# A decoder layer on one core: context column sums made during the K projections, a correction added by VectorE, and another order of issue in the last head pair

## The reference, cut to what matters

```python
x = x + attn(layernorm(x), Wq, bq, Wk, bk, Wv, bv, Wo, bo, gq, gk)   # x: 2 x 256 x 512, 32 heads of 128
# second part: both sides are quantised, then multiplied
q1 = fake_quant(layernorm(x), x1_scale, x1_zp)     # (clip(round(v/s + z), 0, 255) - z) * s
q2 = fake_quant(ctx_4096, x2_scale, x2_zp)         # ctx_4096: 2 x 512 x 512
x = x + matmul(q1, q2)
# third part: base product, router over 15, top 8, eight low-rank experts
x = x + ffn(layernorm(x), base_W, base_b, router_W, router_b, A, B, expert_map)
```

## Time and profile before

| | us |
|---|---|
| median of 3 runs | 529.79 (529.35 to 529.89) |
| the profiled execution | 529.43 |
| its span in the profile | 527.5 |
| PE busy in the span | 516.9 |
| last pair starts on PE | 474.2 |
| last projection of the last pair ends on PE | 493.85 |
| variance of tiles 2 and 3 ready on DVE | 495.70 |
| longest wait of PE behind 474 us | 0.78 |
| low_rank(0) starts on PE | 504.7 |
| last sum on DVE ends | 525.4 |

### The profile page before, as it was taken

One profiled execution on the slowest core, in us unless ns is written; L12 is line 12 of the kernel. 1 busy time (PEld: TensorE's weight loads), 2 busy tenths in 40 slices (PEclk: granted clock), 3 DMA queues, 4 the chain that ended last, 5 costly groups with the idle time before them and its releaser, 6 DMA issues.

```text
span 527.5 us, 9751 instructions
## 1 busy us (share of the span) xinstructions
PE 516.9 (98%) x3195; PEld 459.4 (87%) x3197; DVE 331.9 (63%) x701; ACT 355.4 (67%) x748; POOL 265.1 (50%) x223
## 2 busy tenths in 40 slices
PE   7999999999999999999999999999999999999897
PEld 6888888888888889999999999999999999997586
DVE  6354433276666777666766667666666667767875
ACT  4666666656666767777767777677777777776650
POOL 3344444464445545564656546465464655643350
PEclk9999999999999999999999999999999999999999
DMA  6444635333333121112221111211233312221002
GB/s 185 140 140 153 224 86 174 99 82 101 97 99 99 60 83 56 50 56 61 60 60 51 49 60 60 60 58 42 60 108 96 139 42 61 60 61 41 1 1 81
DMA packets 23496, 43.43 MB, mean 82 GB/s; under 512 B 3633, under 2 KB 3889, under 8 KB 23217
## 3 DMA queue, kind: packets, MB, share of 16 engines
q1 hardware_dynamic: 23472, 43.13, 27.1%
HBM read 41.03 MB, written 2.10 MB: 82 GB/s over the span
## 4 chain that ended last, share of the span: by engine, by line
PE 89%; DVE 5%; ACT 2%; DMA 2%; POOL 1%; issue 0%; SPq 0%; DVEq 0%; ACTq 0%
PE p_v L624 5%; PE p_o L551 5%; PE p_o L549 5%; PE p_o L550 5%; PE p_v L626 5%; PE p_v L625 5%; PE p_t L549 5%; PE p_t L551 5%; PE p_t L550 5%; PE acc L638 5%; PE acc L639 5%; PE acc L640 5%; PE p_t L610 5%; PE p_o L669 3%; PE p_o L671 3%; PE p_o L670 3%
## 5 line engine op out<-in xcount | busy, mean ns | idle before, releaser
L1205 DVE TENSOR_TENSOR w_lo<-raw,w_hi 128x512 fp32r<-128x512 f32 x64 | 44.2, 690 | 78.5 <-ACT w_hi L784 78.5
L1074 POOL TENSOR_TENSOR wo_lo<-raw,wo_hi 128x512 fp32r<-128x512 f32 x31 | 40.2, 1297 | 100.3 <-ACT wo_hi L939 97.1
L861 ACT ACTIVATE probs<-p_s,nbias,rq_t 128x256 f32<-128x256 f32 x128 | 71.2, 560 | 19.4 <-DVE nbias L1305 19.4
L784 ACT CAST w_hi<-raw 128x512 fp32r<-128x512 f32 x64 | 39.9, 624 | 61.0 <-PE p_o L551 29.8
L624 PE MATMUL p_v<-w_hi,xnt_hi 128*128 128x256 f32 x256 | 77.3, 302 | 0.0
L626 PE MATMUL p_v<-w_hi,xnt_lo 128*128 128x256 f32 x256 | 72.3, 282 | 0.0
L625 PE MATMUL p_v<-w_lo,xnt_hi 128*128 128x256 f32 x256 | 72.2, 282 | 0.0
L1056 POOL TENSOR_TENSOR acc_k<-acc_k,square 128x512 f32<-128x512 f32 x32 | 41.6, 1299 | 50.8 <-ACT square L799 50.8
L1056 POOL TENSOR_TENSOR acc_q<-acc_q,square 128x512 f32<-128x512 f32 x32 | 44.3, 1385 | 39.2 <-ACT square L799 38.9
L915 ACT CAST pt_hi<-p_t 128x512 fp32r<-128x512 f32 x64 | 37.4, 584 | 37.7 <-PE p_t L610 37.7
L1074 POOL TENSOR_TENSOR w_lo<-raw,w_hi 128x512 fp32r<-128x512 f32 x32 | 44.8, 1401 | 23.3 <-ACT w_hi L845 23.3
(11 more groups left out here) (286 smaller groups left out, 1473.6 us busy)
## 6 DMA issues: line engine op xcount, KB each, us to landing
raw<-in_wv SPq DMA_DIRECT2D x36, 256.0 KB, 2.6
raw<-in_wk SPq DMA_DIRECT2D x32, 256.0 KB, 2.6
raw<-in_wq SPq DMA_DIRECT2D x32, 256.0 KB, 2.6
raw<-in_wo SPq DMA_DIRECT2D x31, 256.0 KB, 2.6
ctx_f<-in_ctx SPq DMA_DIRECT2D x4, 512.0 KB, 3.7
xin<-in_x SPq DMA_DIRECT2D x4, 256.0 KB, 3.3
xb<-in_x SPq DMA_DIRECT2D x4, 256.0 KB, 5.5
ctx_kept<-ctx_k SPq DMA_DIRECT2D x1, 1024.0 KB, 4.7
```

What stands on the lines that cost most here:

```text
L861: act.activation(probs[:, n, a, :], p_s[:, a, :], ACT.Exp, bias=nbias[:, n, a:a + 1], scale=rq_t[:, 2 * b + a:2 * b + a + 1], accum_out=rs ...
L1074: pool.tensor_tensor(dst, raw[:, slot, :], hi, ALU.subtract).then_inc(w_lo_pool, 1)
L1205: dve.tensor_tensor(w_lo[:, n, 0:NC * DH], raw[:, r, :], w_hi[:, n, 0:NC * DH], ALU.subtract).then_inc(w_lo_dve, 1)
```

## The change

- During the K projections DVE adds the quantised context in pairs of row blocks (`sum_ctx`, 6 adds in all, in its left-over time), and the four `seed_acc` steps move behind them. After the last K unit PE makes the column sums with one matmul per batch (`ones_r` times `ctx_sum`), DVE scales them (`make_corr`) between its first two `weights_lo` of Q, and SP writes them to HBM (`corr_kept`, 512 KB) after eight Q loads. ACT's Q loop is split in two with a wait for that store between. SP loads them back to `corr` behind `ctx_q`.
- The late column sums, `column_part`, `column_lo` and `add_column_part` are gone, and so is ACT's `keep_x1`: DVE `add_correction` writes `acc` + `corr` to `x_res`.
- The last pair is issued in another order on PE, ACT and DVE. Head 31's outputs go to `p_v` (`last_o_bank`), head 30's split halves to tiles of their own (`o_30_hi`, `o_30_lo`). The last projection is split by tile, and the first transpose of q1 stands between its halves.
- The second part uses other banks (`q1t_bank` = `p_s`, `p_t` in turn, `product_bank` = `p_o`, `p_v` in turn). `row_sums`, `base_out(3)`, `low_rank(0)` and `transpose_x3(0)` are at other places on PE, and POOL's `mark_experts` stands behind its last rstd.

```diff
-            with sp.Fori(0, NH // 4) as i:
+            load_heads(wq, 0, NH)
+            load_heads(wq, 1, NH)
+            sp.wait_ge(corr_made, B)
+            sp.dma_start(corr_kept, corr_f[:]).then_inc(corr_kept_out, 16)
+            with sp.Fori(2, NH // 4) as i:
                 load_heads(wq, i, NH)
...
+            sp.wait_ge(corr_kept_out, 16)
+            sp.dma_start(corr[:], corr_kept).then_inc(corr_back, 16)
...
-        def column_sums(pe, b):
...
-        def add_column_part(pe, t):
...
+            pe.wait_ge(ones_r_made, 1)
+            for b in range(B):
+                pe.wait_ge(ctx_summed, b + 1)
+                pe.matmul(p_flat[b], ones_r[:], ctx_sum[:, b, :], start=True, stop=True).then_inc(col_sums_ready, 1)
             project(0, 0, NH)
             project(0, 1, NH)
+            pe.wait_ge(corr_made, B)
...
 
-                for j in range(4):
-                    s = NS - 4 + j
-                    if j < 3:
-                        scores(NH - 2 + (j + 1) % 2, (j + 1) // 2, s + 1)
-                    transpose_probs(s, j % 2)
-                    if j == 0:
-                        v_tile(NP - 1, 3, 1, w_lo_pool, 0, range(NC - 1, NC))
-                    if j == 3:
-                        column_sums(pe, 0)
-                    if j < 2:
-                        project_out(NH - 3, j)
-                    if j > 0:
-                        project_last(j - 1)
-                    if j == 0:
-                        pe.wait_ge(v_lo_done, NH - 1)
-                    if j == 2:
-                        pe.wait_ge(v_lo_done, NH)
-                    probs_v(s, j % 2, j // 2, 1, j % 2)
-                column_sums(pe, 1)
-                project_last(3)
+                s = NS - 4
+                last_scores(s + 1)
+                transpose_probs(s, 0)
+                v_tile(NP - 1, 3, 1, w_lo_pool, 0, range(NC - 1, NC))
+                last_scores(s + 2)
+                pe.wait_ge(v_lo_done, NH - 1)
+                pe.wait_ge(o_lo_done, NH - 2)
+                last_probs_v(s)
+                transpose_probs(s + 1, 1)
+                project_out(NH - 3, 0)
+                pe.wait_ge(v_lo_done, NH)
+                last_probs_v(s + 1)
+                last_scores(s + 3)
+                transpose_probs(s + 2, 0)
+                project_last(0)
+                project_last(1)
+                last_probs_v(s + 2)
+                transpose_probs(s + 3, 1)
+                project_out(NH - 3, 1)
+                pe.wait_ge(o_lo_done, NH)
+                last_probs_v(s + 3)
+                project_last(2)
+                project_last(3, range(0, 1))
+                transpose_q1(pe, 0)
+                project_last(3, range(1, 2))
...
-            transpose_q1(pe, 0)
-            add_column_part(pe, 0)
-            add_column_part(pe, 1)
             quant_product(pe, 0)
             transpose_q1(pe, 1)
             quant_product(pe, 1)
-            add_column_part(pe, 2)
             transpose_q1(pe, 2)
-            add_column_part(pe, 3)
             transpose_q1(pe, 3)
+            transpose_x3(pe, 0)
             quant_product(pe, 2)
-            transpose_x3(pe, 0)
             quant_product(pe, 3)
+            low_rank(pe, 0)
+            transpose_x3(pe, 1)
+            base_out(pe, 0)
+            transpose_x3(pe, 2)
             row_sums(pe)
-            transpose_x3(pe, 1)
-            low_rank(pe, 0)
-            base_out(pe, 0, range(0, 2))
-            transpose_x3(pe, 2)
-            base_out(pe, 0, range(2, NC))
             transpose_x3(pe, 3)
             low_rank(pe, 1)
             low_rank(pe, 2)
             low_rank(pe, 3)
             base_out(pe, 1)
             base_out(pe, 2)
+            base_out(pe, 3, halves=(0,))
...
-            base_out(pe, 3, halves=(0,))
+            base_out(pe, 3, halves=(1,))
...
-                if n == NT:
-                    base_out(pe, 3, halves=(1,))
...
+            with act.Fori(1, 3) as i:
+                for r in range(4):
+                    weights_hi(i, r, NH, NH // 4)
+                    take(i if r >= 2 else i - 1, (r - 2) % 4, NH, q_all, bq_c)
+            act.wait_ge(corr_kept_out, 16)
+            with act.Fori(3, NH // 4) as i:
...
-            def column_part(b):
...
+                s = NS - 4
+                landed = 3 + 2 * (NP - 1)
+                head_out_hi(NH - 2)
+                probs_hi(s)
+                exps(s + 1, 0, 1)
+                v_half_hi(NP - 1, 1, 1)
+                act.wait_ge(w_landed[1], 16 * (NH // 2 + landed))
+                act.copy(wo_30_hi[:], raw[:, 1, :]).then_inc(w_hi_done, 1)
+                last_out_hi(0)
+                probs_hi(s + 1)
+                exps(s + 2, 1, 0)
+                pair_weights_hi(0, 1, 0, landed)
+                last_out_hi(1)
+                probs_hi(s + 2)
+                exps(s + 3, 1, 1)
+                pair_weights_hi(0, 1, 1, landed + 1)
+                probs_hi(s + 3)
+                last_out_hi(2)
                 last_out_hi(3)
...
-            def keep_x1(t):
...
-            column_part(1)
             linear(0)
             linear(1)
             q1_out(0)
-            keep_x1(0)
-            keep_x1(1)
             q1_out(1)
             linear(2)
             linear(3)
-            keep_x1(2)
+            normalise(0)
             q1_out(2)
-            normalise(0)
+            x3_hi(0)
             q1_out(3)
-            x3_hi(0)
-            keep_x1(3)
             normalise(1)
...
-            mark_experts()
+
+            pair_rstd(0)
+            pair_rstd(1)
             for t in range(NT):
                 pool.wait_ge(var_ready, 3 + t)
                 pool.tensor_tensor(rstd[:, t:t + 1], vare[:, t:t + 1], mhalf[:, 0:1], ALU.pow).then_inc(rstd_ready, 1)
+            mark_experts()
...
+            def sum_ctx(b, step):
+
+                if step < 2:
+                    dve.wait_ge(ctx_quantised, 2 * b + step + 1)
+                    n = b * NC + 2 * step
+                    dve.tensor_tensor(ctx_part[:, 2 * b + step, :], ctx_k[:, n, :], ctx_k[:, n + 1, :], ALU.add
+                                      ).then_inc(sum_step, 1)
+                else:
+                    dve.wait_ge(sum_step, 2 * b + 2)
+                    dve.tensor_tensor(ctx_sum[:, b, :], ctx_part[:, 2 * b, :], ctx_part[:, 2 * b + 1, :], ALU.add
+                                      ).then_inc(ctx_summed, 1)
+
+            def make_corr(b):
+
+                dve.wait_ge(col_sums_ready, b + 1)
+                dve.tensor_scalar(corr_f[:, b, :], p_flat[b], qc[:, 3:4], None, ALU.mult).then_inc(corr_made, 1)
...
-                    elif n < 24 and n % 3 == 0:
-                        seed_acc(n // 3 - 4)
+                    elif n < 18:
+                        sum_ctx((n - 12) // 3, n % 3)
+                    elif n < 22:
+                        seed_acc(n - 18)
...
-            for r in range(3):
+            weights_lo(0, 0, NH)
+            make_corr(0)
+            make_corr(1)
+            for r in range(1, 3):
...
+            def add_correction(t):
+
+                if t == 0:
+                    dve.wait_ge(corr_back, 16)
+                dve.wait_ge(linear_done, t + 1)
+                return later(dve.tensor_tensor(x_res[:, t, :], acc[t][:], corr[:, t // 2, :], ALU.add))
+
+            def second_sum(t, n):
+
+                done(n)
...
-            def column_lo(b):
...
-            out_lo(NH - 3)
             slot_max(NS - 3, 0, 1)
             probs_lo(NS - 4)
+            out_lo(NH - 3)
             slot_norm(NS - 3, 1)
 
+            slot_max(NS - 2, 1, 0)
+            v_half_lo(NP - 1, 1, 1)
+            probs_lo(NS - 3)
             last_out_lo(0)
-            slot_max(NS - 2, 1, 0)
-            probs_lo(NS - 3)
             slot_norm(NS - 2, 0)
-            v_half_lo(NP - 1, 1, 1)
-
+
+            slot_max(NS - 1, 1, 1)
             last_out_lo(1)
-            slot_max(NS - 1, 1, 1)
             probs_lo(NS - 2)
+            slot_norm(NS - 1, 1)
+
             stats1(0)
-            slot_norm(NS - 1, 1)
-
-            last_out_lo(2)
-            probs_lo(NS - 1)
             n = stats1(1)
             pair_variance(0, n)
-            column_lo(0)
+            probs_lo(NS - 1)
+            last_out_lo(2)
+            pair_coefficients(0)
             last_out_lo(3)
-            pair_coefficients(0)
-            column_lo(1)
             quantise(0)
+            c0 = add_correction(0)
             stats1(2)
+            quantise(1)
             n = stats1(3)
             pair_variance(1, n)
-            quantise(1)
-            second_sum(0)
+            c1 = add_correction(1)
             pair_coefficients(1)
+            second_sum(0, c0)
             n0 = stats3(0)
             variance3(0, n0)
+            second_sum(1, c1)
             quantise(2)
-            second_sum(1)
             bias3(0)
+            n1 = stats3(1)
             quantise(3)
-            n1 = stats3(1)
             variance3(1, n1)
```

(30 more changed lines are left out.)

120 lines of the change are left out of this document (47 added, 73 removed).

## The result

| us | before | after |
|---|---|---|
| median | 529.78 (20 runs, 529.08 to 530.24) | 530.4 (20 runs, 530.1 to 531.98) |
| the profiled execution, its span | 529.43, 527.5 | 530.25, 528.3 |
| mean granted clock of a run | 0.999 or 1.000 in 87 of 88 runs of the comparisons below | 0.992 to 0.997 in all 20 |

After divided by before is 1.0017 (1.0011 to 1.0023): 0.9 us slower. I had forecast 528.7, 1.05 us faster, in a range of 527.9 to 529.6.

The account below looks back on a forecast made before the run. PE was taken to bound the kernel until 474 us, then waits among all engines, then PE again from low_rank(0). +0.45 - 1.6 + 0.1 = -1.05 us on 529.79 gave 528.74, stated as 528.7, range 527.9 to 529.6.

Parts of the forecast that it names:

- K and Q border: Between K and Q projections: two new 128x512 matmuls on PE cost +0.45 us; scaling, adds, store and load stay hidden.
- Rival 3: At the K/Q border DVE's scaling comes late and PE waits; 529.7 with 1 us lost beyond the cover; chance 0.05.
- Last pair: Last head pair: exponentials start earlier, PE idles 1.5 us before scores(62), then runs full; probs_v(63) 2.0 us earlier, at 488.2.
- So I walk the new order with the old durations: Method behind 474 us: each instruction keeps its old time, the next starting 0.03 to 0.06 us behind what it waits for.
- To the second linear and low_rank(0): From the last projections into the second part: linear(2) 2.9 us earlier, at 495.2, and low_rank(0) 2.45 earlier, at 502.25.
- The walk: Stage-by-stage timing of the new order, the main case: 528.0 to 529.4 us, chance 0.78.
- rival 2: PE's clock falls to 1.2 GHz after idle pauses, doubling matmuls between 498 and 502 us: +3.3, to 532; chance 0.04.
- the first 3 us: Program start, PE busy only 0.38 us at granted clock 1.00: the row used as evidence against rival 2.
- PE's own stretch: low_rank(0) to the transposes of hw: 15.45 us instead of 13.5 as work moves in, ending 0.5 us earlier, at 517.7.
- Outputs: Transposes of hw to the last output sum: five sums back to back, 2.9 us instead of 4.0, gaining 1.1.
- the stores' +0.1: End of the kernel: the last two stores follow within 0.4 us and SP needs about that to issue one: +0.1 us.
- The sum: Whole kernel: +0.45 at the border, -1.6 at the last output sum and +0.1 at the stores give -1.05 us.

Follow-up runs that it names:

- early_only: The kernel before plus only the early sums, two column-sum matmuls, scaling, store and load back, result unused, late column sums kept: 530.35 us, ratio 1.0010 against before.
- pool_later: The changed kernel with POOL's rstd of tiles 0 and 1 before its last w_lo chunk, which waits for DVE's coefficients: 529.74 us, ratio 1.0002 against before.
- end_old: The changed kernel with both halves of base_out(3) back at their places of before: 530.14 us, ratio 1.0009 against before.
- fill8: The changed kernel with eight useless 128x512 matmuls on PE ahead of the third q1 transposes: 529.75 us, ratio 1.0002 against before.
- quant_early: The changed kernel, no fillers, with quantise(2), quantise(3), ACT's q1(2), q1(3) outputs and PE's product(2) issued earlier: 528.86 us, ratio 0.9986 against before.

## Why the prediction was wrong, by its own steps

- **K and Q border, +0.45: right.** Q's first unit is at 97.83 behind the two column sums at 97.37 and 97.60, with no wait; `early_only` measures +0.6 (0.05 to 1.0) for it. Rival 3 did not come.
- **Last pair, probs_v(63) 2.0 earlier: the mechanism right, the size 0.9 too large.** Scores(62) came at 3.1 behind scores(61), to 0.01 us. Then three things. First, 0.6 us went to `vare` beside POOL's `w_lo`. The failed step is "So I walk the new order with the old durations": 0.17 us for `vare` holds only while POOL is not at work beside it, and the new order put the variance beside POOL's chunk, where it took 1.14. `pool_later` gives the 0.6 back. Second, the sum itself is wrong: up to probs_v(63) the new order has three rounds of transposes and not two, and the terms named add up to 10.8, not 10.95. Put right, 10.1 + 0.36 + 0.4 + 0.25 = 11.1, 0.2 more; `pool_later`, without the stall, took 11.17. Third, the cast of `wo_hi` came 4.5 us behind scores(61) instead of 4.0, since its load landed late (0.95 us of waiting, 0.25 in the earlier trace rows). That is worth about 0.1: where POOL's `wo_lo` behind that cast starts 4.99 us behind scores(61) (end_old), probs_v(61) comes 3.64 us behind scores(62); in after it is 5.16 and 3.71, in fill8 5.36 and 3.89.
- **To the second linear and low_rank(0): a further 0.8 lost.** Linear(2) is 0.8 late, all of it from the last pair. low_rank(0) is 1.7 late, and of the 0.8 more `fill8` gives 0.7 back by holding the clock. The walk had the pause ("PE waits over 2 us for quantise(2)", measured 2.14) and counted the matmuls behind it at 1.00: it put the lower clock at nothing. This is the second failed step, and with it the chance of 0.04 for rival 2. It rested on the first 3 us, where PE is busy 0.38 and the clock 1.00: rows from the start of a program did not carry over to a pause in its middle. (The other pause that the rival named, 1.42 us ahead of scores(62), left the clock at 1.00.) The rival's own price of 3.3 us was also wrong: it doubled all matmuls from 498 to 502, but waits that were there anyway took up most of it. The runs show 0.65 (fill8), 1.0 (end_old's runs at one clock and the other) and 1.2 us (quant_early's). The Trainium skill (TensorE: Matmul & The Clock Gate, Part 1: The HAM clock gate), which I had set aside for that row, says that throttled is the default and activity lifts it; by that rule a thin stretch is a risk, and the trace of after agrees, with 0.50 from 501 to 504 us.
- **PE's own stretch, 15.45 us of work: right, but with its cover used up.** 45.4 - 29.7 = 15.7. The walk had hw ready near 516.5, 1.2 us ahead of PE. In after it was ready at 519.66, 0.06 us ahead of the transposes. 1.05 us of the delay is the subtraction of the row maximum (1.27 instead of 0.22), the same failed step as for `vare`; it was hidden here by 0.06 us, and in `end_old`, where PE has 1.45 us less to do ahead of the transposes, it waits 0.57 us for hw.
- **Outputs, 1.1 less: right** (6.1 against 7.2 in `end_old`), **the stores' +0.1 came as +0.4.** The span ends 2.4 to 2.5 us behind the last sum in each kernel with the new end and 2.1 to 2.2 in each with the old. I priced SP's issue alone; why the two stores end later was not tried. Moving base_out(3) is in all worth nothing: 1.45 us ahead of the transposes and 0.4 for the stores stand against 1.1 and a wait for hw.
- **The sum.** Forecast -1.05; 0.9 more in the last pair, 0.8 up to low_rank(0) (0.7 of it the clock), 0.2 in PE's own stretch and 0.3 at the stores make +1.15. The profiled execution shows +0.8, since it came 0.3 us earlier to the K/Q border; the ratio says +0.9 (0.6 to 1.2).

## What to carry to other kernels

Walk a new order with the old durations, but first lay POOL's instructions beside DVE's small SBUF steps: what starts just behind a POOL instruction of 1.3 us can last nearly as long as it. Count the instructions of the new order from the order itself: a round left out was 0.36 us here. When work was taken off PE in a stretch where it already waited, nothing was gained there and the clock was lost for the next matmuls: look for work (or fillers) to put there, or move up what PE waits for. That the clock was at 1.00 while PE stood idle at one end of a program is no evidence for its middle.
